# A four-layer graph network on one core: GpSimd adds x in layer 0's last units, layer 2's residual sums are split over two engines, layer 3's two stages become one

## The chip, the cores and the metric

The kernel runs on one core of one Trainium2 chip. The core has five engines that run their own instruction queues beside each other: TensorE (PE, matrix products), VectorE (DVE), ScalarE (ACT), GpSimd (POOL) and SyncE (SP, which here only starts transfers). They share the on-chip memory SBUF; matrix products land in the eight banks of PSUM. Sixteen DMA engines carry data between memory (HBM) and SBUF. Engines wait for each other by semaphores only. The metric is the device time of one execution in microseconds (us).

## The reference

A graph of 50,000 nodes with 256 numbers each, 25,000 edges sorted by target. Four layers follow each other, each as x = layernorm(x + layer(x)):

```python
x = _layernorm(x + _L0_gnn_ref(x, ..., src, dst))            # exp(clip(k[src].q[dst])) weights, weighted mean of v[src]
x = _layernorm(x + _L1_gnn_ref(x, edge_index, ...))          # sum of neighbours, two-matrix MLP, layernorm, relu
x = _layernorm(x + _L2_gnn_ref(x, edge_index, ...))          # attention over edges and self loops, inner layernorm
x = _layernorm(x + _L3_gnn_ref(x, edge_index, edge_attr_256, ...))
return x

# layer 0
score = jnp.exp(jnp.clip(jnp.sum(k[src] * q[dst], -1, keepdims=True) / np.sqrt(D_K), -5.0, 5.0))
out = segment_sum(v[src] * score, dst) / (segment_sum(score, dst) + 1e-09)

# layer 2, after the attention sum `out`: an inner norm with weights, then the outer one adds x again
y = out + x
return (y - mu) / jnp.sqrt(var + EPS) * ln_w + ln_b

# layer 3
k_j, v_j, q_i = k[src] + e, v[src] + e, q[dst]               # e = edge_attr @ We
alpha = softmax over the edges of one target of sum(q_i * k_j, -1) / sqrt(C)
out = segment_sum(v_j * alpha, dst) + x @ Ws + bs
```

All of it is in float32.

## The kernel before

The program is a row of stages with a barrier of all engines between them: `prepare`, `layer0`, `nodes1` (layer 1), `nodes2` (layer 2), `edges3` and `nodes3` (layer 3). Edges are worked in 196 chunks of 128, nodes in 196 units of 256 (two tiles of 128 rows). A unit fetches the window of edges that point into its rows, and a matrix of zeros and ones (`hot`, built by comparing a row number with each edge's target) sums those edges' messages into the rows by a matrix product.

Inside a stage each engine has its own function, which is called once per step. The step's number minus a lag gives the unit or chunk that an operation belongs to: `at(20)` in step s is unit s-20. So the order of the work on an engine is the order of the lines in its function, and the lags set how many units are in flight. Rings of buffers (`u % 4`, `u % 8`) and semaphores with counted values (`wait_ge(summed, u + 1)`) tie the engines together. GU = 8 units form a group whose softmax is worked at once, in a few steps of each eight.

- `layer0` does two chunks of edges and one unit of nodes in each step. The chunks end in step 99, so steps after that have units only. In those late steps DVE adds 1e-9 to the sums of weights (L782), builds `hot` in two halves (L403), inverts (L810), divides the sums by it (`mean_msg`, L796), adds x (`ln_rows`, L831) and works the layernorm: statistics (L431, L437), inverse root (L447), shift (L451). PE sums the messages (L646), ACT takes the root and applies the norm. SP loads x for units below LATE = 104, and from 104 on GpSimd's queue does (L473), eight units ahead; the load waits until the unit that used the same buffer has its `ln_rows`.
- `nodes2` (layer 2): GpSimd fetches neighbour rows by two indirect transfers a unit (L1210), adds x to `own` (L1217), and adds x to the scaled inner norm (`outer_rows`, L1222). DVE makes `own` (L1359), the inner statistics (L1374), the shift of both norms (L1379), the outer statistics (L1395), the scaling (L1412: PSUM bank `agg` times the row `ln_w`, into `outer_rows`), and `weighted` (L1437). PE may use a bank of `agg` for unit u when `scaled_done` has told that unit u-4 was scaled (L1291).
- `edges3` makes keys, values and scores of the 196 chunks: PE turns (L1615) and multiplies (L1625, L1630), DVE adds biases (L1678), products and sums; results go to `msg3_d`. `kv_ps` has four PSUM banks in turn. `nodes3` then loads windows of `msg3_d`, works the softmax in groups, and from step 18 turns x (L1866), from step 19 multiplies by `w_s` and sums the messages (L1879, L1880).

## Time and profile before

| what | us |
|---|---|
| median of 3 runs | 4782.54 (4775.28 to 4793.21) |
| the profiled execution | 4778.9 |
| its span | 4776.8 |
| busy in the span: PE, DVE, POOL, ACT | 4433.2, 4015.9, 3219.7, 2669.6 |

The span runs from the first to the last instruction; 2.1 us of the execution lie around it. Busy time alone does not tell what sets the time of a stage, since each stage has a different limit. A row of a timeline gives the start and the duration of an instruction; the distance between two starts is what one costs when an engine is full, since an instruction begins before the record of the one ahead ends.

### The profile page before, as it was taken

The page shows a single profiled execution, that of the slowest core. Times are in us where ns is not written, and L with a number is a line of the kernel's source. Part 1 is how long each engine was busy: PE and PEld are TensorE (multiplying, and loading weights), DVE is VectorE, ACT ScalarE, POOL GpSimd, SP SyncE. Part 2 cuts the span into 40 slices and gives each one's busy share as a digit, 9 for nine tenths or more (in the row PEclk, how much of TensorE's full clock was granted, in tenths as well). Part 3 has the DMA queues.
Part 4 walks back from the last instruction along what each step waited for, and adds up shares of the span by engine and source line. Part 5 has one row for each costly group of instructions (what it writes and reads, how often), then busy time and mean ns, then how long its engine had stood idle before and what let it go on. Part 6 is the DMA issues. An engine that isn't in the chain of part 4 may idle for free. (4 is left out here: it accounts for less than half of the span.)

```text
span 4776.8 us, 89771 instructions
## 1 busy us (share of the span) xinstructions
PE 4433.2 (93%) x21134; PEld 3447.4 (72%) x21134; DVE 4015.9 (84%) x12177; ACT 2669.6 (56%) x5893; POOL 3219.7 (67%) x3835
## 2 busy tenths in 40 slices
PE   6999998769999999999978999999869999699999
PEld 4666664438888888888857777777746666488888
DVE  4677778989999999999957888888867777588887
ACT  2788886545555555555545777777731112155555
POOL 5555551237777777777747899999766666288887
PEclk9999996559999999999988999999989999899999
DMA  5977778974444444444447899998855555588886
GB/s 163 240 222 220 223 222 255 297 223 114 152 150 149 153 150 151 151 150 151 149 150 213 260 264 265 263 264 263 252 159 178 175 175 175 150 266 262 259 263 185
DMA packets 911644, 970.43 MB, mean 203 GB/s; under 512 B 104938, under 2 KB 867672, under 8 KB 911306
## 3 DMA queue, kind: packets, MB, share of 16 engines
q1 hardware_dynamic: 501268, 472.10, 33.9%
q10 hardware_dynamic: 327254, 315.21, 19.3%
q0 software_dynamic: 82784, 179.41, 13.6%
q8 instruction: 116, 1.90, 0.2%
q14 instruction: 222, 1.82, 0.1%
HBM read 654.95 MB, written 363.57 MB: 213 GB/s over the span
## 5 line engine op out<-in xcount | busy, mean ns | idle before, releaser
L571 POOL DMA_INDIRECT layer_xg<-in_x,edge_rows x392 | 386.2, 985 | 330.4 <-PE layer_t_ps L613 228.2
L905 POOL DMA_INDIRECT nodes_near_rows<-x_d,nodes_cur x392 | 417.5, 1065 | 238.2 <-POOL nodes_cur L900 170.9
L1585 POOL DMA_INDIRECT edges_xg<-x_d,edge_rows x392 | 377.1, 962 | 207.8 <-PE edges_x_ps L1615 129.8
L1210 POOL DMA_INDIRECT nodes_near_rows<-hh_d,source_row x392 | 394.9, 1007 | 116.6 <-issue 90.7
L1879 PE MATMUL nodes_agg<-w_s,nodes_xT 128*128 128x256 f32 x1568 | 404.8, 381 | 0.9 <-ACT nodes_xT L1900 0.9
L1025 PE MATMUL nodes_h_ps<-w_h,nodes_x2T 128*128 128x272 f32 x1568 | 392.2, 393 | 7.8 <-ACT nodes_x2T L1102 7.8
L1643 ACT ACTIVATE edges_xT<-edges_x_ps 128x512 f32<-128x512 f32 x196 | 117.0, 597 | 487.2 <-PE edges_x_ps L1615 487.2
L646 PE MATMUL layer_agg<-layer_msg,layer_hot 128*128 128x264 f32 x784 | 313.1, 539 | 65.7 <-issue 65.7
L1035 PE MATMUL nodes_hid_ps<-nodes_zT,w_a 128*128 128x256 f32 x1568 | 372.3, 380 | 0.7 <-ACT nodes_zT L1109 0.7
L1015 PE MATMUL nodes_out_ps<-w_b,nodes_hid 128*128 128x256 f32 x1568 | 371.1, 380 | 0.6 <-ACT nodes_hid L1094 0.5
L628 PE MATMUL layer_kv_ps<-w_kv,layer_xT 128*128 128x512 f32 x784 | 370.1, 594 | 0.9 <-DVE layer_made L772 0.9
L1630 PE MATMUL edges_kv_ps<-w_kv,edges_xT 128*128 128x512 f32 x784 | 368.6, 592 | 0.0
L920 POOL TENSOR_TENSOR nodes_x2b<-nodes_x,row_L_gnn_ln_b 128x512 f32<-128x512 f32 x196 | 264.8, 1351 | 142.1 <-DMA x_d<-nodes_x2b 131.1
L1025 PEld LDWEIGHTS nodes_h_ps<-w_h,nodes_x2T 128*128 128x128 f32 x1568 | 297.3, 190 | 65.5 <-ACT nodes_x2T L1102 9.7
L646 PEld LDWEIGHTS layer_agg<-layer_msg,layer_hot 128*128 128x128 f32 x784 | 191.1, 260 | 211.0 <-issue 183.4
L463 ACT ACTIVATE layer_y<-layer_ln_rows,layer_ln_shift,layer_ln_rstd 128x256 f32<-128x256 f32 x392 | 213.8, 592 | 218.8 <-DVE layer_ln_shift L451 218.8
L1035 PEld LDWEIGHTS nodes_hid_ps<-nodes_zT,w_a 128*128 128x128 f32 x1568 | 298.9, 191 | 46.9 <-ACT nodes_zT L1109 1.1
L1879 PEld LDWEIGHTS nodes_agg<-w_s,nodes_xT 128*128 128x128 f32 x1568 | 283.8, 191 | 32.1 <-ACT nodes_xT L1900 1.3
L1015 PEld LDWEIGHTS nodes_out_ps<-w_b,nodes_hid 128*128 128x128 f32 x1568 | 282.6, 190 | 31.3 <-ACT nodes_hid L1094 1.0
L962 DVE SCALAR_TENSOR_TENSOR nodes_scaled<-nodes_inner_rows,nodes_inner_moments,row_L_gnn_gamma 128x256 f32<-128x256 f32 x392 | 304.1, 814 | 0.0
L986 DVE SCALAR_TENSOR_TENSOR nodes_affine<-nodes_scaled,nodes_inner_rstd,row_L_gnn_beta 128x256 f32<-128x256 f32 x392 | 287.5, 772 | 0.1
L1222 POOL TENSOR_TENSOR nodes_outer_rows<-nodes_outer_rows,nodes_xin 128x512 f32<-128x512 f32 x196 | 250.1, 1276 | 53.2 <-DVE nodes_outer_rows L1412 53.2
(233 smaller groups left out, 12645.1 us busy)
## 6 DMA issues: line engine op xcount, KB each, us to landing
nodes_xin<-x_d SPq DMA_DIRECT2D x588, 256.0 KB, 3.5
layer_msg<-msg_d SPq DMA_DIRECT2D x392, 132.0 KB, 3.8
hh_d<-nodes_hh ACTq DMA_DIRECT2D x196, 264.0 KB, 4.0
nodes_msg<-msg_d SPq DMA_DIRECT2D x392, 132.0 KB, 3.3
x_d<-layer_y ACTq DMA_DIRECT2D x196, 256.0 KB, 3.9
x_d<-nodes_x2b ACTq DMA_DIRECT2D x196, 256.0 KB
nodes_hin<-hh_d SPq DMA_DIRECT2D x196, 256.0 KB
x_d<-nodes_x ACTq DMA_DIRECT2D x196, 256.0 KB, 4.5
```

What stands on the lines that cost most here:

```text
L571: gp.indirect_dma_start(out=xg[:, c % 8, k, :], out_offset=None, in_=x, in_offset=bass.IndirectOffsetOnAxis(ap=edge_rows[:, c, k:k + 1], a ...
L628: last = nc.tensor.matmul(kv_ps[b][:, :], xT[:, b, 0, i, :], w0_kv[:, i, :], start=i == 0, stop=i == KC - 1)
L646: last = nc.tensor.matmul(agg[u % 2][:, h, 0:D + H], hot[:, u % 4, h, :], msg[:, r, h, :], start=True, stop=True)
L905: gp.indirect_dma_start(out=near_rows[:, r, h, :], out_offset=None, in_=x1_d, in_offset=bass.IndirectOffsetOnAxis(ap=cur[:, r, h:h + 1], a ...
L962: last = nc.vector.scalar_tensor_tensor(scaled[:, b, h, :], inner["rows"][:, ring(u, 4), h, :], inner["moments"][:, ring(u, 4), h, 0:1], r ...
L1015: last = nc.tensor.matmul(out_ps[ring(u, 2)][:, h * D:(h + 1) * D], hid[:, ring(u, 2), k, h * P:(h + 1) * P], w1_b[:, k, :], start=k == 0, ...
L1025: last = nc.tensor.matmul(h_ps[:, h, 0:D + 2 * H], x2T[:, ring(u, 2), k, h, :], w2_h[:, k, :], start=k == 0, stop=k == KC - 1)
L1035: last = nc.tensor.matmul(hid_ps[:, m * 2 * P:(m + 1) * 2 * P], w1_a[:, k, m * P:(m + 1) * P], zT[:, ring(u, 2), k, :, :].rearrange("p h n ...
L1210: gp.indirect_dma_start(out=near_rows[:, u % NR, h, :], out_offset=None, in_=hh_d, in_offset=bass.IndirectOffsetOnAxis(ap=source_row[:, 2 ...
L1585: gp.indirect_dma_start(out=xg[:, c % 8, k, :], out_offset=None, in_=x3_d, in_offset=bass.IndirectOffsetOnAxis(ap=edge_rows[:, c, k:k + 1] ...
L1630: last = nc.tensor.matmul(kv_ps[r][:, :], xT[:, b, 0, j, :], w3_kv[:, j, :], start=j == 0, stop=j == KC - 1)
L1879: nc.tensor.matmul(to, xT[:, u % 2, k, h, :], w3_s[:, k, :], start=k == 0, stop=False)
```

## The change

1. **Layer 0, units 104 to 195.** After each load of x, GpSimd also adds x to `mean_msg` into `ln_rows`, four units behind the load it has just started, and signals `late_filled`. DVE no longer does this for those units. `mean_msg` has four buffers, two before. In every step, DVE's statistics of a unit now stand behind the next unit's division, and the two halves of `hot` are built in two places, in part a step earlier.
2. **Layer 2.** GpSimd adds x to the outer sum for odd units only. For even units DVE scales in place in the PSUM bank and, as the last work of the step, adds x from the bank into `outer_rows`. PE's bank of an even unit is released by that add.
3. **Layer 3.** `edges3` and `nodes3` are one stage, `layer3`. The unit steps begin at step 178 of the chunk steps and run interleaved with them to the end of the chunks. `kv_ps` has two banks; the four banks of `agg` are those of `q_ps` and `kv_ps`, and x is turned in the banks that turned the edges' rows.

```diff
+def run_then(eng, total, depth, body, begin, units, follow_depth, follow, unroll=8):
...
+    for s in range(head + loops * unroll, begin + units + follow_depth):
+        if s < total + depth:
+            body(fixed(s))
+        if s >= begin:
+            follow(s - begin, lambda lag: s - begin - lag if 0 <= s - begin - lag < units else None)
...
-                for u in range(LATE, UNITS):
-                    load_x(gp, u)
+                for u in range(LATE, UNITS + 4):
+                    if u < UNITS:
+                        load_x(gp, u)
+                    u -= 4
+                    if u >= LATE:
+                        wait_x(gp, u)
+                        gp.wait_ge(divided, u + 1)
+                        gp.wait_ge(ln["normed"], u - 3)
+                        gp.tensor_tensor(ln["rows"][:, u % 4, :, :], mean_msg[:, u % MEANS, :, :], xin[:, u % 8, :, :], ALU.add)\
+                          .then_inc(late_filled, 1)
...
                     u = at(21)
-                    if u is not None:
+                    if u is not None and u % 2:
                         scaled = outer_rows[:, u % 4, :, :]
                         gp.wait_ge(scaled_done, u + 1)
-                        gp.tensor_tensor(scaled, scaled, xin[:, u % XR, :, :], ALU.add).then_inc(outer_filled, 1)
+                        gp.tensor_tensor(scaled, scaled, xin[:, u % XR, :, :], ALU.add).then_inc(outer_filled[1], 1)
...
-                        if u >= 4:
+                        if u >= 4 and u % 2:
                             pe.wait_ge(scaled_done, u - 3)
+                        elif u >= 4:
+                            pe.wait_ge(outer_filled[0], (u - 4) // 2 + 1)
...
+                    u = at(21)
+                    if u is not None and u % 2 == 0:
+                        ve.wait_ge(scaled_done, u + 1)
+                        ve.wait_ge(x_in[u % XR], u // XR * 16 + 16)
+                        if u >= 4:
+                            ve.wait_ge(outer_normed, u - 3)
+                        nc.vector.tensor_tensor(outer_rows[:, u % 4, :, :], in_halves(agg[u % 4]), xin[:, u % XR, :, :], ALU.add)\
+                            .then_inc(outer_filled[0], 1)
...
-        kv_ps = [ps(f"kv_ps{k}") for k in range(4)]
+        kv_ps = [ps(f"kv_ps{k}") for k in range(2)]
...
+        agg, root_ps = q_ps + kv_ps, x_ps
...
+        BEGIN = EC - 18
...
-                        if had(c, 4):
-                            pe.wait_ge(joined, num(c) - 3)
+                        if had(c, 2):
+                            pe.wait_ge(joined, num(c) - 1)
...
-                run_steps(pe, EC, 2, body)
...
+                run_then(pe, EC, 2, body, BEGIN, UNITS, 19, units)
```

DVE in the late steps of layer 0, one unit before (statistics are BN_STATS and BN_AGGR):

```order
L447 RECIPROCAL layer_ln_rstd<-layer_ln_dev 128x2
L782 TENSOR_SCALAR layer_den<-layer_agg 128x16
L403 TENSOR_SCALAR layer_hot<-iota,target_rel 128x128 x2
L810 RECIPROCAL layer_den<-layer_den 128x16
L451 SCALAR_TENSOR_TENSOR layer_ln_shift<-layer_ln_moments,layer_ln_rstd 128x2
L431 BN_STATS layer_ln_parts<-layer_ln_rows 128x6 x2
L796 TENSOR_TENSOR layer_mean_msg<-layer_agg,layer_den 128x512
L437 BN_AGGR layer_ln_moments<-layer_ln_parts 128x2 x2
L831 TENSOR_TENSOR layer_ln_rows<-layer_mean_msg,layer_xin 128x512
```

and one unit of the changed kernel at the same place:

```order
L464 RECIPROCAL layer_ln_rstd<-layer_ln_dev 128x2
L818 TENSOR_SCALAR layer_den<-layer_agg 128x16
L773 TENSOR_SCALAR layer_hot<-iota,target_rel 128x128
L849 RECIPROCAL layer_den<-layer_den 128x16
L468 SCALAR_TENSOR_TENSOR layer_ln_shift<-layer_ln_moments,layer_ln_rstd 128x2
L831 TENSOR_TENSOR layer_mean_msg<-layer_agg,layer_den 128x512
L448 BN_STATS layer_ln_parts<-layer_ln_rows 128x6 x2
L773 TENSOR_SCALAR layer_hot<-iota,target_rel 128x128
L454 BN_AGGR layer_ln_moments<-layer_ln_parts 128x2 x2
```

The row that wrote `layer_ln_rows` has left DVE; the division stands ahead of the statistics.

GpSimd in layer 2, two units of the changed kernel (before, every unit had all three rows):

```order
L1252 DMA nodes_near_rows<-hh_d,source_row 128x264 x2
L1259 TENSOR_TENSOR nodes_own<-nodes_own,nodes_xin 128x512
L1252 DMA nodes_near_rows<-hh_d,source_row 128x264 x2
L1259 TENSOR_TENSOR nodes_own<-nodes_own,nodes_xin 128x512
L1264 TENSOR_TENSOR nodes_outer_rows<-nodes_outer_rows,nodes_xin 128x512
```

The sum into `nodes_outer_rows` is there once in two units; DVE has the other (L1503).

PE at the end of layer 3's chunks, before:

```order
L1625 MATMUL edges_q_ps<-w_q,edges_xT 128x256 x2
L1630 MATMUL edges_kv_ps<-w_kv,edges_xT 128x512 x2
L1578 UNCONDITIONAL_BRANCH
L1848 UNCONDITIONAL_BRANCH
L1858 MATMUL nodes_score_ps<-ident,nodes_score 128x128
L1888 MATMUL nodes_share_ps<-ident,nodes_share 128x128
L1858 MATMUL nodes_score_ps<-ident,nodes_score 128x128
L1866 MATMUL nodes_xT_ps<-ident,nodes_xin 128x128 x8
L1879 MATMUL nodes_agg<-w_s,nodes_xT 128x256 x2
```

and in the changed kernel (here `layer_q_ps` also holds the unit sums):

```order
L1746 MATMUL layer_x_ps<-ident,layer_xg 128x128 x4
L1756 MATMUL layer_q_ps<-w_q,layer_xT 128x256 x2
L1761 MATMUL layer_kv_ps<-w_kv,layer_xT 128x512 x2
L1772 MATMUL layer_score_ps<-ident,layer_score 128x128
L1782 MATMUL layer_x_ps<-ident,layer_xin 128x128 x4
L1756 MATMUL layer_q_ps<-w_q,layer_xT 128x256 x2
L1761 MATMUL layer_kv_ps<-w_kv,layer_xT 128x512 x2
L1782 MATMUL layer_x_ps<-ident,layer_xin 128x128 x4
L1799 MATMUL layer_q_ps<-w_s,layer_rootT 128x256 x2
L1800 MATMUL layer_q_ps<-layer_weighted,layer_hot 128x256
```

The two branches with the barrier between them are gone, and the first unit's turning stands ahead of the last chunk's products.

## Rows read from the trace of the kernel before

**Rows 1.** Busy time in stretches of layers 0, 2 and 3 (its units):

```profile
core 0: us, PE busy (x) PEld busy (x) DVE busy (x) ACT busy (x) POOL busy (x), PEclk, DMA share, GB/s
850.00:860.00 10.00, 7.63 (x16) 4.05 (x15) 10.00 (x46) 5.32 (x12) 2.89 (x4) 0.50 0.93 286
...
2900.00:3100.00 200.00, 182.05 (x1088) 152.88 (x1089) 178.85 (x580) 147.90 (x351) 180.45 (x161) 1.00 0.91 263
...
4400.00:4600.00 200.00, 200.00 (x1064) 176.51 (x1063) 162.42 (x452) 109.92 (x212) 166.47 (x393) 1.00 0.85 260
```

**Rows 2.** Timeline of DVE in layer 0's late steps; start us, duration us:

```profile
850.99 0.68 DVE L796 TENSOR_TENSOR layer_mean_msg<-layer_agg,layer_den 128x512 f32<-128x512 f32 x1
...
853.00 0.10 DVE L451 SCALAR_TENSOR_TENSOR layer_ln_shift<-layer_ln_moments,layer_ln_rstd 128x2 f32<-128x2 f32 x1
...
853.68 0.68 DVE L796 TENSOR_TENSOR layer_mean_msg<-layer_agg,layer_den 128x512 f32<-128x512 f32 x1
...
854.42 0.67 DVE L831 TENSOR_TENSOR layer_ln_rows<-layer_mean_msg,layer_xin 128x512 f32<-128x512 f32 x1
855.00 0.16 DVE L447 RECIPROCAL layer_ln_rstd<-layer_ln_dev 128x2 f32<-128x2 f32 x1
```

**Rows 3.** The same steps: timeline of POOL and PE:

```profile
850.00 0.72 POOL L473 DMA_DIRECT2D layer_xin<-in_x  x1 [1.97 <-DVE layer_ln_rows L831]
...
851.77 2.10 PE L646 MATMUL layer_agg<-layer_msg,layer_hot 128*128 128x264 f32 x4 [0.59 <-issue]
```

**Rows 4.** Transfers, 850 to 1000 us: line, issues, size, median us to landing:

```profile
layer_msg<-msg_d SPq DMA_DIRECT2D x112, 132.0 KB, 4.4
layer_xin<-in_x POOLq DMA_DIRECT2D x56, 256.0 KB, 4.4
x_d<-layer_y ACTq DMA_DIRECT2D x56, 256.0 KB, 4.3
```

**Rows 5.** Busy time in an early stretch of those steps:

```profile
780.00:790.00 10.00, 7.63 (x16) 4.04 (x15) 10.00 (x46) 5.30 (x12) 2.91 (x4) 0.50 1.04 369
```

**Rows 6.** Timeline of POOL in layer 2:

```profile
2905.33 1.28 POOL L1217 TENSOR_TENSOR nodes_own<-nodes_own,nodes_xin 128x512 f32<-128x512 f32 x1
2906.55 1.28 POOL L1222 TENSOR_TENSOR nodes_outer_rows<-nodes_outer_rows,nodes_xin 128x512 f32<-128x512 f32 x1
2907.99 1.01 POOL L1210 DMA_INDIRECT nodes_near_rows<-hh_d,source_row  x1 [0.16 <-issue]
...
2910.33 1.28 POOL L1217 TENSOR_TENSOR nodes_own<-nodes_own,nodes_xin 128x512 f32<-128x512 f32 x1
...
2931.60 1.27 POOL L1222 TENSOR_TENSOR nodes_outer_rows<-nodes_outer_rows,nodes_xin 128x512 f32<-128x512 f32 x1
```

**Rows 7.** DVE in layer 2, 2700 to 3300 us; busy us, mean ns, idle before:

```profile
L1359 DVE SCALAR_TENSOR_TENSOR nodes_own<-nodes_own_ps,nodes_hin 128x512 f32<-128x512 f32 x120 | 82.3, 686 | 48.2 <-PE nodes_own_ps L1326 48.2
...
L1379 DVE SCALAR_TENSOR_TENSOR nodes_shift<-nodes_moments,nodes_rstd 128x4 f32<-128x4 f32 x120 | 61.2, 510 | 0.0
```

**Rows 8.** Timeline of DVE in layer 2:

```profile
2910.59 0.69 DVE L1359 SCALAR_TENSOR_TENSOR nodes_own<-nodes_own_ps,nodes_hin 128x512 f32<-128x512 f32 x1 [0.18 <-PE nodes_own_ps L1326]
...
2917.14 0.68 DVE L1359 SCALAR_TENSOR_TENSOR nodes_own<-nodes_own_ps,nodes_hin 128x512 f32<-128x512 f32 x1
...
2922.12 0.69 DVE L1359 SCALAR_TENSOR_TENSOR nodes_own<-nodes_own_ps,nodes_hin 128x512 f32<-128x512 f32 x1 [1.37 <-PE nodes_own_ps L1326]
...
2931.95 0.95 DVE L1379 SCALAR_TENSOR_TENSOR nodes_shift<-nodes_moments,nodes_rstd 128x4 f32<-128x4 f32 x1
```

**Rows 9.** Timeline of PE from the last chunk to the third unit of layer 3:

```profile
4123.07 1.88 PE L1630 MATMUL edges_kv_ps<-w_kv,edges_xT 128*128 128x512 f32 x4
...
4165.05 1.92 PE L1866 MATMUL nodes_xT_ps<-ident,nodes_xin 128*128 128x128 f32 x8
...
4173.17 0.64 PE L1866 MATMUL nodes_xT_ps<-ident,nodes_xin 128*128 128x128 f32 x4
```

**Rows 10.** Waits in the chunks, 3600 to 4000 us: us in total, times, longest:

```profile
DVE edges_kv_ps L1678 <- PE edges_kv_ps L1630: 79.5, 133, 0.6
```

## What the change was predicted to do

> **What bounds the kernel now.** I read the busy times by stretch first [rows 1], since no engine is the limit all through, and then in each stage the timeline of the engine that is full or periodic.
>
> In layer 0's late steps DVE is busy 10.00 of 10 us and PE runs at the granted clock of 0.50, the lower of its two levels (1.2 GHz), with PE busy 7.63 [rows 1]. One unit takes 853.68 - 850.99 = 2.69 us on DVE, without a gap [rows 2]. GpSimd issues a load in 0.72 us and then idles 1.97 us until DVE's sum with x lets it go on [rows 3]. DVE is the bound; the reader should see that every instruction there is worth its distance to the next start. But the transfers are near: their share is 0.93 at 286 GB/s [rows 1].
>
> In layer 2 all of PE, DVE and POOL look alike (182, 179 and 180 of 200 us, [rows 1]). The timeline tells them apart: POOL repeats itself in 2910.33 - 2905.33 = 5.00 us whatever the others do [rows 6], 120 units in 600 us [rows 7], while DVE's steps vary between 4.98 and 6.55 us around a group's softmax [rows 8]. DVE also waits 48.2 us for PE in those 600, and its small shift (L1379) has a mean of 510 ns [rows 7] where the same kind of instruction takes 0.10 us in layer 0 [rows 2]. So DVE has slack and POOL sets 5.00 us a unit.
>
> In layer 3's units PE is busy 200 of 200 us at full clock [rows 1]. In its chunks DVE waits for PE 133 times in 400 us, which is one chunk in 3.01 us, PE-bound [rows 10]. Between them stands a hole: the last product of the chunks ends at 4123.07 + 1.88 = 4124.95, the first unit's turning starts at 4165.05, and two units then take 8.12 us, to 4173.17 [rows 9].
>
> **Part 1, layer 0's late units: 92 units (104 to 195).** DVE loses one sum: 855.00 - 854.42 = 0.58 us [rows 2]. The rest of its row is the same work in another order, so its floor is 2.69 - 0.58 = 2.11 us a unit. What is late next?
> - PE: four matmuls in 2.10 us at the low clock [rows 3]; these overlap, so it can just follow; if the clock rises it is free.
> - POOL: the load, 0.72 [rows 3], and a sum of 128x512, which this trace has only in layer 2: 2906.55 - 2905.33 = 1.22 us between starts, with 0.16 us ahead of a transfer's row [rows 6]. Together 2.10, a few hundredths more for its three waits: about 2.15.
> - Transfers: two windows of 132 KB, a load and a store of 256 KB each [rows 4], 776 KB or 794.6 thousand bytes a unit. The fastest stretch moved 369 GB/s (share 1.04, [rows 5]): 2.15 us a unit. Scaling the steady 286 GB/s at share 0.93 to a full share gives 308 GB/s: 2.58 us. The fastest stretch is real traffic of this mix and not scaled, so the truth should lie near it.
>
> Four floors between 2.10 and 2.15 do not meet without loss; I take 2.28 us. Gain 92 x (2.69 - 2.28) = 38 us; ends 92 x (2.69 - 2.58) = 10 and 92 x (2.69 - 2.13) = 52.
>
> The Trainium skill (DMA: Bandwidth & Descriptors, § Bandwidth) puts memory traffic of one core at about 358 GB/s. By it a unit would cost 2.22 us and the gain be 43 us; the stretch at 369 is slightly above it.
>
> The order matters too. After a division DVE does statistics (L431), half of `hot`, merge, inverse, den, the other half, inverse, shift and the next division before it wants this unit's new rows: over 2.1 us, against 1.22 for the sum and up to 0.72 for a load in front of it. So DVE should not wait for `late_filled`. If the statistics stood ahead of the division it would. In the steps before, PE-bound with both chunks and unit, the reordering is hidden by PE and costs nothing; exposed, it would only be one semaphore more.
>
> **Part 2, layer 2: 196 units.** POOL loses a sum in every second unit: 5.00 - 1.25/2 = 4.38 us a unit (1.25 between the 1.22 and 1.28 of [rows 6]). DVE gets it, in even units: 0.59, like the other 128x512 sums (L831 is 0.58, [rows 2]), 0.30 a unit. DVE's present work is 178.85/200 x 5.00 = 4.47 us a unit [rows 1], of which L1379's stretch is (510 - 140)/1000 = 0.37 [rows 7]; 4.10 real, 4.40 with the new sum. PE is at 182/200 x 5.00 = 4.55 including overlap.
>
> Three floors of 4.4 to 4.55, and steps that are not even: around a group one step takes 2917.14 - 2910.59 = 6.55 and the next 4.98, of which 1.37 is a wait for PE that follows the softmax [rows 8]. POOL has no say in those two. Before, DVE made them up while POOL went on at 5.00. Now it has less to make up with: two steps at 6.55 and 4.98, the six others at 4.25 to 4.5, is 11.53 + 6 x 4.45 = 38.2 us for eight, 4.78 a unit.
>
> To this comes the stretch of L1379. At 2931.95 it took 0.95 us and ended at 2932.90; POOL's sum had run from 2931.60 to 2932.87 [rows 6, 8]. A small shift that ends when GpSimd's sum ends is blocked by it, not slow. It is free now, since POOL is the bound. Afterwards POOL sums 1.5 x 1.22 = 1.83 us in 4.8, so with luck left out it is hit in 38% of units and loses half a sum, 0.6: up to 0.23 us a unit. The two engines fall into step with each other, so I take a fifth of it: 4.82. Gain 196 x (5.00 - 4.82) = 35 us. Ends: 4.55 (88 us) and 5.05 (a loss of 10).
>
> The Trainium skill (SBUF — State Buffer, § Who interferes with whom) says that a VectorE instruction with two SBUF inputs and a GpSimd one that reads SBUF block each other completely; the trace agrees with the row above. By that rule the new sum on DVE, with one input in PSUM, is not blocked, and layer 0's shift is.
>
> **Part 3, layer 3.** The hole of 4165.05 - 4124.95 = 40.1 us goes, and with it the slow first units: 8.12 against two at 3.05 (16.25 matmuls a unit, 1064 in 200 us, [rows 1]), 2.0 us. What filled the hole (24 windows, the first group's softmax) now lies under 18 chunk steps of 3.01 us with DVE free 0.6 us in each [rows 10]. Nearly all is in steps with slack; I leave 2 us for stumbles. Two banks of `kv_ps` instead of four: PE may write a bank two chunks later when DVE has joined it. PE's next product into it ends two chunks, 6.02 us, after `kv_done` and takes 1.7 of these, so there are 4.3 us; DVE's whole round is under 3.01. No wait. Gain 40 us; ends 25 and 44.
>
> **Sum.** 38 + 35 + 40 = 113 us. The profiled execution was 4778.9, so 4666; the median of the runs shown is 3.6 above it, so the time of the changed kernel is 4782.5 - 113 = about 4669 us.
>
> **Rivals.**
> - *A: in layer 0 GpSimd's sum blocks DVE's other reads* (both halves of `hot` and the shift). For it: [rows 8] shows a block. Against it: `hot` reads one tile and a scalar, and the shift comes 1.5 us after the division, when the sum of 1.22 should be over. Each block costs up to 0.6: 2.69 again, 4669 + 38 = 4707. Chance 0.10.
> - *B: layer 2 stays at 5.0*, because group steps and the block eat all that POOL gives back. For it: two of eight steps are over POOL's new pace. Time 4669 + 35 = 4704. Chance 0.15.
> - *C: layer 2 gets to PE's 4.55* as the buffers even the steps out. Gain 88 instead of 35: 4616. For it: PE is busy 0.91 and can run a step ahead. Against: the 1.37 us wait. Chance 0.15.
> - *D, slower than before: the even banks.* PE gets an even unit's bank not at the scaling but at the last instruction of DVE's step, about 1.5 us later. If PE then waits and DVE waits for PE's `own` product in turn, a pair of units runs in series. The kernel is slower once layer 2 loses more than parts 1 and 3 give, 78 us, and the 0.5% below, 24 us: 102/98 = 1.04 us a pair, 11.04 against 10.00. Time then 4807 or more. Against it: DVE's end of step and PE's wish for the bank are about level, so the series is short. Chance 0.02.
> - The joined stage does not close the hole because SP's loads or the rings delay the first units: 4669 + 20 = 4689, chance 0.05.
>
> My forecast has 0.53. The range 4605 to 4718 holds C, A and B and leaves out D and sums of several misses. Under 0.5% (24 us) cannot be told from no change. Faster: all but D and a heap of A, B and the last: 0.95. Same 0.02, slower 0.03.
>
> **What would show it.** Layer 0's late units at 2.2 to 2.4 us with DVE no longer at 10.00 of 10, or with the clock up; 2.69 means A. Layer 2 at 4.7 to 4.9 us a unit, POOL idle in front of its sums and DVE without waits outside the group's steps; a fixed period on POOL of 4.38 would mean C or better, waits of PE for DVE's L1503 mean D. No PE gap over 3 us at the joint, the granted clock at 1.00 through it, and chunks still at 3.01 us. I am wrong if layer 2 moves by more than 60 us or layer 0 by less than 10.

## The result and the profile after

| | kernel before | changed kernel |
|---|---|---|
| median of the runs, us | 4779.58 | 4906.05 (4900.14 to 4912.12) |
| ratio | 1 | 1.0261, 95% interval 1.0246 to 1.0275 |
| profiled execution / its span, us | 4778.9 / 4776.8 | 4906.77 / 4905.1 |

The median of before is here that of four runs; the table ahead of the prediction has three of them. The changed kernel is slower by 126 us, where 113 us of gain were forecast. The stretches that answer to [rows 1], with the same columns:

```profile
950.00:960.00 10.00, 6.32 (x14) 3.54 (x13) 8.85 (x34) 4.16 (x9) 5.82 (x7) 0.50 0.75 227
...
3000.00:3200.00 200.00, 176.58 (x1003) 148.43 (x1001) 168.78 (x546) 134.78 (x321) 141.68 (x126) 0.93 0.80 243
4500.00:4700.00 200.00, 200.00 (x1066) 176.52 (x1065) 161.98 (x453) 109.84 (x213) 167.05 (x393) 1.00 0.86 263
```

Layer 3's units stand as before. In layer 0's late steps no engine is full any more, in layer 2 all four are less busy than before, and the transfers move less (0.75 and 0.80 of their time against 0.93 and 0.91). A stage where everything is less busy and that takes longer has a chain of waits in it. By stage, each counted from its first indirect load: layer 1 begins 72 us later (1125.3 against 1052.8), layer 2 takes 92 us more (1148 against 1056), and layer 3 takes 1218 us instead of 1254. That is 128 us in all, the difference of the two spans.

**Layer 0.** Timeline of DVE, ACT and POOL in one late unit of the changed kernel (start, duration, engine, line; in brackets the idle time before and who ended it); it answers to [rows 2, 3]:

```profile
951.31 0.69 DVE L831 TENSOR_TENSOR layer_mean_msg<-layer_agg,layer_den 128x512 f32<-128x512 f32 x1
...
951.92 0.74 DVE L448 BATCH_NORM_STATS2 layer_ln_parts<-layer_ln_rows 128x6 f32<-128x256 f32 x2
...
952.15 1.26 POOL L607 TENSOR_TENSOR layer_ln_rows<-layer_mean_msg,layer_xin 128x512 f32<-128x512 f32 x1 [1.39 <-issue]
952.58 0.92 DVE L773 TENSOR_SCALAR layer_hot<-iota,target_rel 128x128 f32<-128x128 f32 x1
...
953.42 0.23 DVE L454 BATCH_NORM_AGGREGATE layer_ln_moments<-layer_ln_parts 128x2 f32<-128x6 f32 x2
953.68 0.29 ACT L459 ACTIVATE layer_ln_dev<-layer_ln_moments,eps_ln 128x2 f32<-128x2 f32 x1 [1.20 <-DVE layer_ln_moments L454]
954.01 0.17 DVE L464 RECIPROCAL layer_ln_rstd<-layer_ln_dev 128x2 f32<-128x2 f32 x1 [0.36 <-ACT layer_ln_dev L459]
954.10 0.15 DVE L818 TENSOR_SCALAR layer_den<-layer_agg 128x16 f32<-128x16 f32 x1
954.17 0.28 DVE L773 TENSOR_SCALAR layer_hot<-iota,target_rel 128x128 f32<-128x128 f32 x1
...
954.64 0.69 DVE L831 TENSOR_TENSOR layer_mean_msg<-layer_agg,layer_den 128x512 f32<-128x512 f32 x1
```

A unit takes 954.64 - 951.31 = 3.33 us. The same comparison takes 0.28 us at 954.17 and 0.92 at 952.58; the long one ends at 953.50, 0.09 after GpSimd's sum (952.15 + 1.26 = 953.41). The profile counts a blocked instruction as busy, so nothing is listed as a wait. Behind it the merge (L454), ACT's root and the inverse (L464) stand in line with 0.36 us of idle time. In the kernel before, the merge and the root at the same place were:

```profile
854.27 0.25 DVE L437 BATCH_NORM_AGGREGATE layer_ln_moments<-layer_ln_parts 128x2 f32<-128x6 f32 x2
...
854.55 0.30 ACT L442 ACTIVATE layer_ln_dev<-layer_ln_moments,eps_ln 128x2 f32<-128x2 f32 x1 [0.24 <-DVE layer_ln_moments L437]
```

DVE's sum with x (854.42 to 855.00, [rows 2]) filled the time of the root.

**Layer 2.** The step behind a group's shares in the changed kernel, timeline of all four engines; [rows 6, 8] are its counterpart:

```profile
3026.19 1.63 DVE L1423 SCALAR_TENSOR_TENSOR nodes_shift<-nodes_moments,nodes_rstd 128x4 f32<-128x4 f32 x1
3026.52 1.27 POOL L1259 TENSOR_TENSOR nodes_own<-nodes_own,nodes_xin 128x512 f32<-128x512 f32 x1
...
3027.86 0.99 ACT L1552 ACTIVATE nodes_agg<-nodes_agg,nodes_shift,nodes_rstd 128x256 f32<-128x256 f32 x2 [1.89 <-DVE nodes_shift L1423]
...
3029.90 0.30 PE L1361 MATMUL nodes_share_ps<-ident,nodes_share 128*128 128x128 f32 x1 [2.40 <-issue]
...
3030.73 1.02 PE L1370 MATMUL nodes_own_ps<-nodes_own_first,nodes_hot 128*128 128x8 f32 x4 [0.37 <-ACT nodes_own_first L1599]
...
3031.79 0.69 DVE L1403 SCALAR_TENSOR_TENSOR nodes_own<-nodes_own_ps,nodes_hin 128x512 f32<-128x512 f32 x1 [1.26 <-PE nodes_own_ps L1370]
```

GpSimd's sum of `own` falls on the shift (1.63 us instead of 0.15), ACT's norm of the bank waits 1.89 us for it, DVE's scaling and `weighted` come late, and PE, which wants both, idles 2.40 us. Then its clock falls; stretches ahead of this gap and behind it (columns as in [rows 1], the third from the right is the granted clock):

```profile
3022.00:3029.00 7.00, 4.42 (x25) 3.39 (x25) 7.00 (x20) 3.34 (x9) 5.57 (x5) 1.00 0.71 181
3031.00:3036.00 5.00, 5.00 (x18) 4.00 (x19) 3.62 (x13) 2.53 (x5) 1.84 (x2) 0.50 0.48 157
```

At 0.50, the lower level, PE is full (5.00 of 5) and DVE waits for it. The fall lasts 6.8 us and comes in each group. A group is read from the instruction that makes its shares (count, durations in ns, first and last start in 2700 to 3300 us). In the kernel before:

```profile
L1445 DVE TENSOR_TENSOR nodes_share<-nodes_score_ps,nodes_total x15: 277/281/287, 2716.0 to 3277.1; 128x128 f32<-128x128 f32 x15
```

In the changed kernel:

```profile
L1489 DVE TENSOR_TENSOR nodes_share<-nodes_score_ps,nodes_total x14: 272/275/279, 2713.6 to 3290.3; 128x128 f32<-128x128 f32 x14
```

(3277.1 - 2716.0)/14 = 40.08 us for eight units against (3290.3 - 2713.6)/13 = 44.36, or 5.01 against 5.55 a unit. POOL waits for DVE in it. The longest waits of 2800 to 3400 us (total, times, longest):

```profile
POOL nodes_outer_rows L1264 <- DVE nodes_outer_rows L1457: 122.3, 54, 3.1
DVE nodes_own L1403 <- PE nodes_own_ps L1370: 80.4, 71, 3.2
```

**Layer 3.** PE through the joint (the first unit is turned at 4290.05), which answers to the hole of [rows 9]; from 4250 to 4330 us PE is busy 79.33 of 80 us at a granted clock of 1.00:

```profile
4288.22 1.88 PE L1761 MATMUL layer_kv_ps<-w_kv,layer_xT 128*128 128x512 f32 x4
4289.94 0.27 PE L1772 MATMUL layer_score_ps<-ident,layer_score 128*128 128x128 f32 x1
4290.05 0.60 PE L1782 MATMUL layer_x_ps<-ident,layer_xin 128*128 128x128 f32 x4
```

### The profile page after: what moved, and what is told of

The parts are those of the page before. It is cut to its first block and busy times, and to the rows that moved or that the text cites. A ratio compares the mean times of both kernels' runs of the same rounds, so it can differ in the third digit from the quotient of the medians.

```text
span 4905.1 us, 90498 instructions
## 1 busy us (share of the span) xinstructions
PE 4484.4 (91%) x21134; PEld 3486.4 (71%) x21134; DVE 4086.9 (83%) x12183; ACT 2663.1 (54%) x5893; POOL 3234.9 (66%) x3829
## 5 line engine op out<-in xcount | busy, mean ns | idle before, releaser
L596 POOL DMA_INDIRECT layer_xg<-in_x,edge_rows x392 | 403.8, 1030 | 324.9 <-PE layer_t_ps L646 222.6
L1676 POOL DMA_INDIRECT layer_xg<-x_d,edge_rows x392 | 376.9, 962 | 201.3 <-PE layer_x_ps L1746 132.9
L1821 ACT ACTIVATE layer_xT<-layer_x_ps 128x512 f32<-128x512 f32 x196 | 117.0, 597 | 485.0 <-PE layer_x_ps L1746 485.0
L661 PE MATMUL layer_kv_ps<-w_kv,layer_xT 128*128 128x512 f32 x784 | 370.0, 594 | 0.8 <-DVE layer_made L808 0.8
L1761 PE MATMUL layer_kv_ps<-w_kv,layer_xT 128*128 128x512 f32 x784 | 369.6, 594 | 0.0
L1264 POOL TENSOR_TENSOR nodes_outer_rows<-nodes_outer_rows,nodes_xin 128x512 f32<-128x512 f32 x98 | 124.7, 1273 | 259.6 <-DVE nodes_outer_rows L1457 259.6
L1136 ACT ACTIVATE nodes_hid<-nodes_hid_ps,b 128x256 f32<-128x256 f32 x392 | 164.8, 471 | 190.8 <-PE nodes_hid_ps L1077 190.8
L955 POOL TENSOR_TENSOR nodes_xb<-nodes_xin,row_L_gnn_b 128x512 f32<-128x512 f32 x196 | 250.1, 1276 | 24.8 <-DVE nodes_inner_rows L988 21.3
```

The lines of the kernel that those rows point to most:

```text
L596: gp.indirect_dma_start(out=xg[:, c % 8, k, :], out_offset=None, in_=x, in_offset=bass.IndirectOffsetOnAxis(ap=edge_rows[:, c, k:k + 1], a ...
L661: last = nc.tensor.matmul(kv_ps[b][:, :], xT[:, b, 0, i, :], w0_kv[:, i, :], start=i == 0, stop=i == KC - 1)
L1676: gp.indirect_dma_start(out=xg[:, c % 8, k, :], out_offset=None, in_=x3_d, in_offset=bass.IndirectOffsetOnAxis(ap=edge_rows[:, c, k:k + 1] ...
L1761: last = nc.tensor.matmul(kv_ps[r][:, :], xT[:, b, 0, j, :], w3_kv[:, j, :], start=j == 0, stop=j == KC - 1)
```

## The experiments

Runs sent together share a chip and its runs of the kernel before. On the third set's chip that kernel takes 4822 us instead of 4779, so totals are compared by ratio and stages with runs of the same set.

### The parts apart

Three kernels take one part each, word for word out of the change: `join_only` part 3, `l0_only` part 1, `l2_only` part 2.

> The kernel before with part 3 alone: layer 3's chunks and units in one stage, layers 0 and 2 untouched. The trace of the changed kernel has layer 3 at 1191 us against 1239, so if the parts are independent this takes about 4780 - 46 = 4734 us. If the join were what disturbs the other layers, it would come out at 4779 or above.

> The kernel before with part 1 alone: the sum with x on GpSimd in layer 0's last 98 units, the statistics behind the next division, half of hot apart. Layer 0 took 72 us more in the changed kernel, so if the parts are independent this takes about 4780 + 72 = 4852 us, the late units at 3.33 us each and GpSimd's sum ending together with DVE's second half of hot. If the loss in layer 0 came from the other layers' tables or buffers, it would come out near 4740.

> The kernel before with part 2 alone: in layer 2 DVE adds x in the even units. If the parts are independent this takes about 4780 + 94 = 4874 us, 5.55 us a unit, with one fall of the granted clock to 0.50 in each group of eight units. If layer 2 only lost because layer 0 shifted phases or heated the clock's budget, it would come out near 4745.

| | us | ratio to before (95%) | against 4779.25 |
|---|---|---|---|
| join_only | 4741.26 | 0.9928 (0.9911 to 0.9944) | -38 |
| l0_only | 4848.03 | 1.0144 (1.0127 to 1.0161) | +69 |
| l2_only | 4868.18 | 1.0188 (1.0171 to 1.0205) | +89 |

The sum is +120, the change measured +126: within 6 us the parts are independent. The join gives 38 us where the prediction had 40. The expectation's 46 came of stage lengths of 1239 and 1191 us; counted from the stage's first indirect load they are 1254 and 1218, 36 less, and in `join_only` 1218 too. The expectation of `l0_only` speaks of 98 units; GpSimd adds in 92, from unit 104 on. `l2_only` has 44.35 us a group, `l0_only` the 3.33 us a unit. The last scaling of a chunk (`layer_made`), with count, durations, first and last start, in `l2_only`, whose layer 0 is that of before:

```profile
L772 DVE TENSOR_TENSOR layer_made<-layer_kv_ps,layer_made x196: 418/425/426, 52.4 to 758.2; 128x256 f32<-128x256 f32 x196
```

The same in `l0_only`:

```profile
L785 DVE TENSOR_TENSOR layer_made<-layer_kv_ps,layer_made x196: 417/425/426, 52.6 to 772.9; 128x256 f32<-128x256 f32 x196
```

From the first to the last of them 720.3 us pass in `l0_only`, 705.8 in `l2_only` and 706.5 in `join_only`. So of layer 0's 70 us, about 14 are lost in the early steps, where the reordering was called free.

### Layer 0: `hot` moved out of GpSimd's sum (l0_away)

```diff
 def late(s, at):        # steps from 112 on; part 1 before
-    # division, statistics, half of hot, merge, inverse, den, half of hot, reciprocal, shift
+    # division, statistics, merge, den, inverse, reciprocal, shift, both halves of hot
```

> Part 1 alone, and from the first step that has no chunk DVE works in another order: den, inverse of the statistics, reciprocal, shift, both halves of hot, division, statistics, merge. Both halves then stand behind the shift, when GpSimd's sum has ended, and GpSimd's sum falls on the statistics and the merge. Theory that the two engines block each other at SBUF: no half of hot over 0.35 us, the late units at 2.5 to 2.6 us instead of 3.33, and 65 to 75 us less than part 1 alone. Rival, that the loss comes of GpSimd's period or of the transfers, whatever DVE does meanwhile: still 3.2 to 3.4 us a unit. Rival, that only ACT's root behind the late statistics costs: that wait remains here (0.3 us a unit or more), 2.9 to 3.0 us.

4813.84 us, ratio 1.0071 (1.0054 to 1.0087) against 1.0144 for part 1 alone. Timeline of DVE and POOL:

```profile
902.28 0.47 DVE L750 TENSOR_SCALAR layer_hot<-iota,target_rel 128x128 f32<-128x128 f32 x2
...
903.27 0.74 DVE L425 BATCH_NORM_STATS2 layer_ln_parts<-layer_ln_rows 128x6 f32<-128x256 f32 x2
...
903.50 1.26 POOL L584 TENSOR_TENSOR layer_ln_rows<-layer_mean_msg,layer_xin 128x512 f32<-128x512 f32 x1 [0.84 <-issue]
904.15 0.25 DVE L431 BATCH_NORM_AGGREGATE layer_ln_moments<-layer_ln_parts 128x2 f32<-128x6 f32 x2
...
905.04 0.48 DVE L750 TENSOR_SCALAR layer_hot<-iota,target_rel 128x128 f32<-128x128 f32 x2
```

A unit takes 905.04 - 902.28 = 2.76 us, 0.57 less, and both halves together 0.47, as in the kernel before. Statistics under GpSimd's sum keep their 0.74. The rival of a fixed period of GpSimd or the transfers (3.2 to 3.4) is out, and so is the one that only ACT's root costs (2.9 to 3.0). The number 2.5 to 2.6 is missed: the inverse still waits 0.31 us for ACT's root, and the merge directly behind the statistics starts 0.88 us after them, where another instruction starts 0.66 after them. The median is only 34 us below part 1 alone, where 65 to 75 were expected. In this profiled execution (4833 us) layer 1 begins 48 us earlier than in `l0_only` (1075.0 against 1122.9), but layer 2 took 33 us more, with the same instructions; that is used below.

### Layer 0: the same order, `iota` read from PSUM (l0_psum)

```diff
-    return nc.vector.tensor_scalar(hot[:, u % 4, h, :], iota[:, :], target_rel[...], None, ALU.is_equal)
+    return nc.vector.tensor_scalar(hot[:, u % 4, h, :], q_ps[:, D:D + P] if u >= LATE else iota[:, :], target_rel[...], None, ALU.is_equal)
```

> Part 1 alone, DVE's order unchanged, but from unit 98 on both halves of hot are compared from a copy of iota that lies in a PSUM bank instead of SBUF. Half of hot still stands in GpSimd's sum. Theory that the two block each other at SBUF when both read it: this half takes about 0.3 us instead of 0.92, the late units 2.6 to 2.75 us instead of 3.33, total about 4848 - 92 x 0.63 = 4790 us. Rival, that anything DVE does there is held until GpSimd's sum ends (an order of semaphores, or a port taken for writing as well): 0.92 and 3.33 stay, 4848 us.

4805.55 us, ratio 1.0057 (1.0038 to 1.0076). Timeline of POOL and DVE:

```profile
900.59 1.26 POOL L584 TENSOR_TENSOR layer_ln_rows<-layer_mean_msg,layer_xin 128x512 f32<-128x512 f32 x1 [0.87 <-issue]
901.02 0.33 DVE L750 TENSOR_SCALAR layer_hot<-layer_q_ps,target_rel 128x128 f32<-128x128 f32 x1
...
901.88 0.17 DVE L441 RECIPROCAL layer_ln_rstd<-layer_ln_dev 128x2 f32<-128x2 f32 x1 [0.36 <-ACT layer_ln_dev L436]
```

Only the place of one operand was changed, and the comparison in the middle of GpSimd's sum takes 0.33 us instead of 0.92. That settles it: GpSimd's sum blocks DVE's reading of SBUF by this instruction. A unit takes 2.81 us, a little over the 2.6 to 2.75 expected; the root's 0.36 us is left. Unblocked, a half costs 0.26 us from start to start out of PSUM and 0.19 out of SBUF (954.36 - 954.17).

The Trainium skill (SBUF — State Buffer, § Who interferes with whom) names `tensor_scalar` among the operations that can enter a two-port mode and then contend with GpSimd, where the one that comes second is blocked for the whole instruction of the other. The trace agrees: the comparison, a `tensor_scalar` with one tensor as input, ends 0.09 us after GpSimd's sum when it reads SBUF and runs through when it reads PSUM. That DVE blocks GpSimd in turn is not seen here; GpSimd's sum takes 1.26 us on average in all these runs. The prediction had drawn on that section for the two-input shift alone.

### Layer 0: den and `hot` under ACT's root (l0_best)

```diff
+    # PSUM copy of iota; late steps: den, both halves of hot, reciprocal, inverse, shift, division, statistics, merge
```

> As the run with iota in PSUM, and DVE's order in steps without chunks is den, both halves of hot, reciprocal, inverse of the statistics, shift, division, statistics, merge, so that den and hot lie between the merge and the inverse that waits for ACT's root. The run with the halves of hot moved away showed 2.77 us a unit with 0.31 us of wait for the root left in it. Theory: that wait goes too, 2.45 to 2.5 us a unit, total about 4848 - 92 x 0.85 = 4770 us. Rival, the transfers (share 0.94 at 2.77 us) hold the unit at 2.58 to 2.7 us: 4780 to 4790 us.

4790.15 us, ratio 1.0024 (1.0011 to 1.0038). Statistics and merge on DVE:

```profile
903.35 0.74 DVE L425 BATCH_NORM_STATS2 layer_ln_parts<-layer_ln_rows 128x6 f32<-128x256 f32 x2
...
904.24 0.25 DVE L431 BATCH_NORM_AGGREGATE layer_ln_moments<-layer_ln_parts 128x2 f32<-128x6 f32 x2
```

The wait for the root is gone, the unit takes 2.62 us and no transfer is waited for. The expected 2.45 to 2.5 were missed, and 2.62 is where the rival of the transfers (2.58 to 2.7) had put it; the next run, with 2.41, shows that they do not hold it. No wait is listed for DVE either, and 0.89 us pass from the start of the statistics to that of the merge. Statistics and merge next to each other cost DVE 0.2 us that its row of before did not have.

### Layer 0: a third order, and the early steps as before (l0_final)

```diff
+    # steps from 112 on, iota in PSUM: half of hot, merge, den, other half, reciprocal, inverse, shift, division, statistics
+    # steps before 112: both halves together and statistics ahead of the division, as before
```

> Part 1 alone in a third form. The steps that still have chunks run in DVE's order of before (both halves of hot together, statistics ahead of the division). In the steps without chunks the order is half of hot, merge, den, the other half, reciprocal, inverse, shift, division, statistics, with iota in PSUM. Theory: the instruction behind the statistics is no longer the merge that needs them (0.89 us from start to start there, 0.66 ahead of a half of hot), and the merge has 0.65 us of other work behind it until the inverse needs ACT's root: 2.35 to 2.45 us a unit, and the chunks end at 752 us as before instead of 764. Total about 4780 - 92 x 0.29 = 4753 us. Rival, the transfers hold the unit at 2.55 to 2.65 (share 0.95 at 2.62 us): 4775 us. Rival on the early steps, that the four buffers of mean_msg or GpSimd's program and not DVE's order made the chunks late: they end at 764 again, 10 us more.

4806.65 us against 4822.18, ratio 0.9960 (0.9940 to 0.9981), which is 19 us of 4780. DVE from one division to the next:

```profile
901.26 0.69 DVE L785 TENSOR_TENSOR layer_mean_msg<-layer_agg,layer_den 128x512 f32<-128x512 f32 x1
...
901.87 0.74 DVE L425 BATCH_NORM_STATS2 layer_ln_parts<-layer_ln_rows 128x6 f32<-128x256 f32 x2
...
902.53 0.34 DVE L750 TENSOR_SCALAR layer_hot<-layer_q_ps,target_rel 128x128 f32<-128x128 f32 x1
902.78 0.24 DVE L431 BATCH_NORM_AGGREGATE layer_ln_moments<-layer_ln_parts 128x2 f32<-128x6 f32 x2
...
903.41 0.14 DVE L441 RECIPROCAL layer_ln_rstd<-layer_ln_dev 128x2 f32<-128x2 f32 x1
...
903.67 0.69 DVE L785 TENSOR_TENSOR layer_mean_msg<-layer_agg,layer_den 128x512 f32<-128x512 f32 x1
```

The row of 900 to 950 us, columns as in [rows 1]:

```profile
900.00:950.00 50.00, 36.97 (x84) 20.91 (x82) 48.95 (x230) 28.16 (x62) 40.09 (x42) 0.65 1.03 335
```

A unit takes 2.41 us, as expected, and DVE is the bound; the transfers move 335 GB/s without anybody waiting for them. The chunks end at 782.0 us against 781.5 in `l2_ownfill` (layer 0 as before, same chip): DVE's order had made them late, not the buffers. Layer 1 begins 22.8 us earlier than there (1049.2 against 1072.0), and its first statistics 26.9 us (1075.7 against 1102.6), where 27 were expected. Falls of the clock in layer 2 gave a part of that back in this profile: at a mean of 0.93 the stage takes 1084 us, against 1064 at 0.96 in `join_l0fill`. Which of the moved instructions costs the early steps was not tried apart.

### Layer 2: GpSimd's sum of `own` first (l2_ownfirst)

```diff
+    u = at(17)   # wait own_done, x_in; own += x
     u = at(0)    # two indirect loads
-    u = at(17)   # wait own_done, x_in; own += x
```

> Part 2 alone, and in each step of GpSimd's program the sum of own with x stands ahead of the two indirect loads instead of behind them. Theory that layer 2 is slow because this sum falls on DVE's shift in the step behind the shares, and PE then idles 2.4 us: the sum ends before the shift begins, a group of eight units takes 38.5 to 40 us instead of 44.4, total about 4868 - 24.5 x 5 = 4745 us. Rival, that DVE's extra sum of 0.59 us in even steps is itself what lengthens the group: 44 us stay. Rival, that the loads, now later, make the shares late: 45 us or more.

4788.51 us, ratio 1.0009 (1.0000 to 1.0019) against 1.0188 for part 2 alone. POOL and DVE in the step behind the shares:

```profile
2995.39 1.27 POOL L1207 TENSOR_TENSOR nodes_own<-nodes_own,nodes_xin 128x512 f32<-128x512 f32 x1
...
2997.59 0.15 DVE L1381 SCALAR_TENSOR_TENSOR nodes_shift<-nodes_moments,nodes_rstd 128x4 f32<-128x4 f32 x1
```

The sum is over before the shift. A group takes 41.0 us instead of 44.4: most of the loss was this collision and its weaker kin (the shift's mean falls from 435 to 211 ns in 2700 to 3300 us), neither DVE's extra sum nor the transfers. The 38.5 to 40 expected were missed, and the clock still falls once in each group, now for 3.4 us.

### Layer 2: PE's gap filled (l2_fill)

```diff
                         pe.wait_ge(share_ready, g + 1)
+                        for k in range(5):      # unread products
+                            nc.tensor.matmul(score_ps[:, 0:D], ident[:, :], w3_e[:, 0, :], start=True, stop=True)
```

> Part 2 alone, and PE issues five more matmuls of 128x256, whose product nobody reads, in each group where it otherwise idles 2.4 us behind the shares. They add no wait, and PE has the time. Theory that the fall of the granted clock to 0.50 behind this gap costs on top of the gap: no fall in layer 2's groups, the group at 41 to 42.5 us instead of 44.4, total about 4868 - 24.5 x 2.5 = 4805 us. Rival, that the gap alone costs and the slow stretch is hidden by DVE: the clock stays up and the group still takes 44 us. Rival, that the fall has nothing to do with the gap: it stays.

4835.81 us, ratio 1.0107 (1.0089 to 1.0125), two fifths of the loss in total back. A group takes 43.14 us, where 41 to 42.5 were expected; the granted clock in 2900 to 3100 us is 0.98 against 0.91 in `l2_only`, with falls of 3.4 us in about every second group. One of those left comes behind another gap of PE, which was not filled:

```profile
2927.31 0.44 PE L1279 MATMUL nodes_work_ps<-ident,nodes_hot 128*128 128x128 f32 x2 [1.56 <-ACT nodes_e_row L1537]
```

So the fall depends on PE's gaps and costs beside them. The size is not clean, because GpSimd's sums met the shift longer here, three times in each group for 1.6 to 1.9 us (2900 to 3100 us; count, busy us, mean ns):

```profile
L1383 DVE SCALAR_TENSOR_TENSOR nodes_shift<-nodes_moments,nodes_rstd 128x4 f32<-128x4 f32 x37 | 29.0, 784 | 0.0
```

The clean price comes from two profiles with the same instructions in layer 2. 3000 to 3200 us in `l0_away`:

```profile
3000.00:3200.00 200.00, 182.23 (x1051) 152.98 (x1052) 162.26 (x551) 140.56 (x337) 173.14 (x154) 0.95 0.86 254
```

The same stretch in the kernel before:

```profile
3000.00:3200.00 200.00, 182.05 (x1089) 152.91 (x1089) 178.85 (x581) 147.77 (x351) 180.48 (x161) 1.00 0.91 264
```

With one fall of 3.4 us in each group it takes 41.9 us, without 40.08: 1.8 us. The gap ahead of the shares is itself longer with the fall. PE in `l0_away`:

```profile
2999.54 0.30 PE L1369 MATMUL nodes_share_ps<-ident,nodes_share 128*128 128x128 f32 x1 [0.91 <-issue]
```

and in the kernel before:

```profile
3000.84 0.30 PE L1317 MATMUL nodes_share_ps<-ident,nodes_share 128*128 128x128 f32 x1 [0.56 <-issue]
```

So the 1.8 us are the price of the fall together with what it delays. Why one execution keeps falling and another does not is open.

### Layer 2: both (l2_ownfill), and all together (best, join_l0fill)

> Part 2 alone with GpSimd's sum of own ahead of the indirect loads, and with four unread matmuls of 128x256 for PE in the gap ahead of the shares. The run with the order alone had 41.05 us a group with a fall of the clock in each; the kernel before has 40.08 without falls and, in the run with hot moved away in layer 0, 41.9 with a fall in each group. Theory that the fall costs 1.2 to 1.8 us a group: 39.2 to 39.9 us a group, no falls, total 4740 to 4765 us. Rival, that the new order of the sums is itself the bound and the fall is a companion: 41 us stay, 4788 us.

> All three parts: layer 3 joined, layer 0 in the third form, layer 2 with GpSimd's sum of own first and the four unread matmuls. If the parts stay independent: 4780 - 38 (join) - 27 (layer 0) - 10 to - 25 (layer 2) = 4690 to 4705 us. If layer 2's form is no better than before: 4715 to 4735.

> Layer 3 joined, layer 0 in the third form, layer 2 as before but with the four unread matmuls ahead of the shares. It tells what part 2 adds at all. Theory that before's layer 2 is bound by GpSimd's 5.00 us a unit and loses only in executions with falls of the clock: 40.1 us a group, no falls, 4712 to 4720 us. Rival, that the matmuls cost PE time: 40.5 to 41 us a group, 4725 to 4740.

| | us | ratio to before (95%) | group in layer 2 |
|---|---|---|---|
| l2_ownfill | 4801.97 | 0.9955 (0.9940 to 0.9970) | 39.69 |
| best | 4738.42 | 0.9828 (0.9815 to 0.9841) | 39.68 |
| join_l0fill | 4751.25 | 0.9852 (0.9837 to 0.9867) | 40.04 |

Shares in `best`, where the clock stays at 1.00 from 2527 to 3492 us:

```profile
L1525 DVE TENSOR_TENSOR nodes_share<-nodes_score_ps,nodes_total x15: 280/284/287, 2707.0 to 3262.5; 128x128 f32<-128x128 f32 x15
```

Four unread matmuls take the group of `l2_ownfirst` from 41.0 to 39.69 us (on another chip, but before's group is the same 40.0 to 40.1 us on both) and the falls out of it; so the fall was a cost, not a companion. The unread matmuls do nothing else: `join_l0fill` has before's layer 2 with them, and its 40.04 us are before's 40.08 without falls. Against that, part 2 with the new order of GpSimd is worth 0.36 us a group, 9 us in all (13 between the totals). GpSimd is no longer the bound: its longest wait in `best`, 2700 to 3300 us, is

```profile
POOL nodes_outer_rows L1298 <- DVE nodes_outer_rows L1493: 68.6, 45, 1.9
```

Which chain sets the 39.7 us instead of the 38.6 forecast (8 x 4.82) was not taken apart. Both combined kernels are faster than before, `best` by 84 us (1.7%), on this chip; scaled to 4780 that is 4698 us, within the 4690 to 4705 expected. `join_l0fill` scales to 4709, just below its 4712 to 4720.

## Why the prediction was wrong

- **Which engine bounds.** Right for before: freeing DVE in layer 0 and closing PE's hole in layer 3 was worth about 23 and 38 us once the side effects were gone. GpSimd's part in layer 2 is borne out more weakly: without falls its 5.00 us a unit stand in every run that keeps its sums, but taking 0.62 us a unit from it gave 0.05, 9 us in all.
- **Part 1, forecast +38 us of gain, measured a loss of 69.** The step that failed: "The rest of its row is the same work in another order, so its floor is 2.69 - 0.58 = 2.11". The row of 3.33 us has 1.22 more than that. About 0.65 is the half of `hot` (953.42 - 952.58 = 0.84 against 0.19) blocked by GpSimd's sum. 0.36 is the wait for ACT's root: the removed sum had covered it, and the list of what is late next (PE, POOL, transfers) left ACT out. Of the remaining 0.2 about 0.1 is the division, which now starts right when the reciprocal that feeds it ends (954.36 + 0.25 = 954.61, L849), where before the statistics lay between; the rest is the merge, which nothing overlaps any more. Rival A named the block, but at one end of its range (2.69) and with a chance of 0.10: "Against it: `hot` reads one tile and a scalar". `l0_psum` shows that argument false. The shift, held to be the one in danger, was not hit.
- **"In the steps before ... the reordering is hidden by PE and costs nothing"**: about 14 us; `l0_final`, with the old order there, does not lose them.
- **"So DVE should not wait for `late_filled`"**: right. The transfers: right that 2.58 was no floor; 2.41 us were reached at 335 GB/s.
- **Part 2, forecast +35, measured a loss of 89.** The step that failed: "with luck left out it is hit in 38% of units and loses half a sum ... The two engines fall into step with each other, so I take a fifth of it". The size of the hits was about right, their place had no term. GpSimd waits for DVE's scaling (122.3 us above), so its program is tied to DVE's. In all eight groups between 2800 and 3200 us the shift takes 1.63 us 2.1 us behind the shares, 0.60 and 0.52 at two later places, and 0.13 to 0.19 at the other five. In the kernel before the hits had fixed places too, but other ones: 0.14 us behind the shares, and 0.34 to 0.96 in five of the steps 11 to 31 us later. That the longest hit now lies in the step ahead of PE's longest wait made its gap of 0.56 us into one of 2.40, and the clock fell behind it; with the sum moved away from there a group was 3.4 us shorter. The mean duration of the shift even fell (408 ns against 512 in 2900 to 3100 us): where it is long counts, not how often. The granted clock was 1.00 in [rows 1] and had no term in the sum.
- **Part 3, forecast +40, measured 38**: right in place and size. Rivals B, C and D did not come about: PE waits for the even bank (L1503) twice in the whole of layer 2, both times in its last 50 us, 3.9 us together. The kernel is slower by another path than D's, and slower had 0.03.
- With the block, the root, the collision and the falls taken away the forecast's gains come back in a smaller size: 2.41 us (2.28 forecast, 2.69 before) and 4.96 us a unit (4.82 forecast, 5.01 before). For layer 2 that is a quarter of the gain, and why it is no more stays open.

## What to carry to other kernels

Work that goes from DVE to GpSimd is not gone from DVE: list what DVE does in the time of GpSimd's instruction, and ask of each whether it reads two tensors from SBUF or is a `tensor_scalar` on SBUF; an operand in PSUM, or another order, frees it. When an instruction is taken out of a full engine, ask which short chains through another engine it had covered. And an engine that stops being the bound starts to follow another one; then its collisions move to other fixed places in the period, so a chance per unit is the wrong measure, and it has to be asked which places they are and who waits there.

## What the runs showed of the hardware that I had not expected

- A comparison of 128x128 fp32 with a scalar per row takes 0.28 us from SBUF, 0.92 when GpSimd's 128x512 sum runs, and 0.33 from PSUM whether it runs or not. BATCH_NORM_STATS2 on SBUF is not disturbed (0.74 for two).
- The merge that reads the statistics just written starts 0.88 us after they start; another instruction in between starts after 0.66.
- The same stage, with the same instructions, ran with a fall of the granted clock in every group (`l0_away`) or with none (before, 2700 to 3300 us), 41.9 against 40.08 us a group and 33 us in the stage. The falls came behind PE's gap ahead of the shares, 0.91 us long there and 0.56 in before; four unread matmuls of 128x256 in it took them away.
- In layer 0's late steps at 2.41 us a unit the clock went up and down (0.65 on average) where it had stayed at 0.50 at 2.69, with no effect on the time, since DVE bounds.
